# Four cross-attention layers on one core: the next group's projections moved into a PSUM bank of their own ahead of the feed-forward, and attention outputs produced transposed in 32-column strips

## What is computed

```python
# layer 0: per token, heads mix with heads; relu feed-forward, norm after each sum
# layer 1: quantised attention (queries, keys, weights and values rounded to 8 bits)
x = x + qattn(ln(x), ln(x)); x = x + qattn(ln(x), ctx); x = x + geglu_ffn(ln(x))
# layer 2: norm after each sum
logits = qh @ kh.T / sqrt(16) + mask * -1e9
attn1 = mha(x, x, x, look_ahead);       out1 = ln(x + attn1)
attn2 = mha(ctx, ctx, out1, padding);   out2 = ln(out1 + attn2)
x = ln(out2 + relu(out2 @ w1 + b1) @ w2 + b2)
# layer 3: norm ahead of each part
x = x + attn(ln(x), ctx, mask=None)
x = x + attn(ln(x), ln(x), mask=drop)   # masked keys get -inf
x = x + gelu(ln(x) @ w1 + b1) @ w2 + b2
```

## Time and profile before

| | |
|---|---|
| runs | 2275.02, 2273.48, 2274.74 us; median 2274.74 |
| profiled execution | 2274.92 us, span 2273.2 us |
| mean granted TensorE clock | 0.899 of full speed |
| TensorE matmul busy | 1921.8 us, 85% of the span |
| VectorE busy | 1307.1 us, 57% |
| ScalarE busy | 967.8 us, 43% |
| GpSimd busy | 996.9 us, 44% |

### The profile page before, as it was taken

One profiled execution on the slowest core, in us unless ns is written; L12 is line 12 of the kernel. 1 busy time (PEld: TensorE's weight loads), 2 busy tenths in 40 slices (PEclk: granted clock), 3 DMA queues, 4 the chain that ended last, 5 costly groups with the idle time before them and its releaser, 6 DMA issues.

```text
span 2273.2 us, 32499 instructions
## 1 busy us (share of the span) xinstructions
PE 1921.8 (85%) x10497; PEld 1507.4 (66%) x10497; DVE 1307.1 (57%) x2218; ACT 967.8 (43%) x2274; POOL 996.9 (44%) x1235
## 2 busy tenths in 40 slices
PE   4666667677887887887999899998988999999997
PEld 3565556454664655664777677777766787787776
DVE  5877778658558558658444465454533635436361
ACT  1111221224334333334546465564644665556563
POOL 5566665535335336345333454434533423333330
PEclk8889998677877887887999999999988999999999
DMA  7100000000200000000000200000000000000000
GB/s 216 69 5 5 9 5 5 5 1 6 79 1 5 5 0 5 5 0 5 6 1 6 79 0 9 0 5 5 1 5 5 6 6 0 5 23 0 9 1 10
DMA packets 31292, 34.88 MB, mean 15 GB/s; under 512 B 3196, under 2 KB 30040, under 8 KB 30808
## 3 DMA queue, kind: packets, MB, share of 16 engines
q1 hardware_dynamic: 31192, 33.70, 4.8%
HBM read 31.60 MB, written 2.10 MB: 15 GB/s over the span
## 4 chain that ended last, share of the span: by engine, by line
PE 60%; DVE 11%; issue 4%; POOL 2%; ACT 2%; DVEq 0%; POOLq 0%; ACTq 0%
PE ps L503 31%; PE ps L670 9%; PE ps L701 8%; PE ps L680 6%; PE ps L514 3%; DVE xn L874 2%; DVE rowmax L1010 1%; DVE rowsum L1016 1%; PE ps L696 1%; PE ps L668 1%; DVE work L1012 1%; DVE work L1004 1%; DVE O L845 1%; POOL x_all L1126 1%; DVE stats L864 0%
## 5 line engine op out<-in xcount | busy, mean ns | idle before, releaser
L503 PE MATMUL ps<-hT,w_slot 128*128 128x256 f32 x1856 | 455.1, 399 | 21.1 <-ACT hT L744 21.1
L503 PEld LDWEIGHTS ps<-hT,w_slot 128*128 128x128 f32 x1856 | 359.7, 199 | 77.8 <-ACT hT L744 24.0
L1190 POOL TENSOR_TENSOR work<-KT,own_head 128x512 f32<-128x512 f32 x256 | 261.5, 1047 | 288.6 <-ACT KT L756 234.3
L680 PEld LDWEIGHTS ps<-ident,work 128*128 128x128 f32 x1536 | 206.4, 154 | 178.3 <-issue 110.6
L670 PE MATMUL ps<-work,QT 128*128 128x512 f32 x512 | 276.5, 622 | 22.8 <-POOL work L1190 20.6
L680 PE MATMUL ps<-ident,work 128*128 128x128 f32 x1536 | 265.5, 301 | 35.6 <-POOL work L1199 35.6
L1199 POOL TENSOR_SCALAR work<-work,winv 128x128 f32<-128x128 f32 x512 | 184.9, 384 | 218.9 <-DVE winv L1029 218.4
L886 DVE TENSOR_TENSOR x_all<-ps,x_all 128x512 f32 (+1 forms) x88 | 60.7, 690 | 379.6 <-PE ps L503 326.9
L829 ACT ACTIVATE work<-work,rowmax 128x128 f32<-128x128 f32 x768 | 245.0, 392 | 68.1 <-DVE rowmax L1008 66.5
L701 PEld LDWEIGHTS ps<-V,work 128*128 128x128 f32 x2048 | 251.2, 192 | 7.4 <-issue 4.4
L701 PE MATMUL ps<-V,work 128*128 128x17 f32 x2048 | 248.9, 254 | 2.4 <-ACT work L818 2.4
(11 more groups left out here) (119 smaller groups left out, 3015.6 us busy)
## 6 DMA issues: line engine op xcount, KB each, us to landing
ctx_in<-in_ctx SPq DMA_DIRECT2D x32, 256.0 KB, 2.7
w_slot<-in_L_xattn_W SPq DMA_DIRECT2D x2, 1024.0 KB, 6.4
w_slot<-in_L_xattn_ff_w SPq DMA_DIRECT2D x1, 2048.0 KB, 11.2
w_slot<-in_L_xattn_ffn_w SPq DMA_DIRECT2D x2, 1024.0 KB, 9.9
w_slot<-in_L_xattn_w SPq DMA_DIRECT2D x2, 1024.0 KB, 9.3
out<-x_all SPq DMA_DIRECT2D x8, 256.0 KB, 2.1
x_all<-in_x SPq DMA_DIRECT2D x1, 1536.0 KB, 11.7
pad<-in_mask_Bx1x1xS_fk SPq DMA_DIRECT2D x1, 1024.0 KB, 6.7
```

The lines of the kernel that those rows point to most:

```text
L503: mm = pe.matmul(dst, lhsT(k), rhs(k), start=(k == 0), stop=(k == chunks - 1))
L680: mm = pe.transpose(bank(2 + u % 2)[:, tok(h)], prob[u % NP][:, tok(h)], ident[:, :])
L1190: pool.tensor_tensor(KB[u % NK].rearrange("p (h k) -> p h k", h=HU), keys, own_head[:, half * HU:(half + 1) * HU].unsqueeze(2).broadcast_t ...
```

## The change

**Transposed outputs (`direct`), in layers 2 and 3.** The values step now takes 32 columns of a zero-padded `Vz` (two heads of a pair, the other's columns zero) as weights and streams 128 columns of the transposed exponentials: four f32 matmuls per unit that go in turn to two 32-column strips of the array, into one bank (`o_bank`, bank 4) for both sequences. What comes out is transposed already, so `ot` and its copy are gone. Nothing sums the weights any more: VectorE gets a reduction over 128x512 for each unit (`row_sums`, line 1099), one reciprocal of 128x32 and one copy of it to 128x512 columns (lines 1104, 1112), TensorE transposes that (`inverse_rows`, line 751, four transposes at step 11), ScalarE copies it to `inv_T` at step 12, and VectorE multiplies bank 4 by it at step 12 (line 1121, 128x512). `turn(0)` of the next phase waits for `inv_T_ready`. In the quantised layer the two scalings of 128x256 become one of 128x512 at step 12.

**The next group's start, in layers 1 to 3.** `join` is replaced by `ending`: the next group's pieces are put at fixed early slots, in bank 5 (`third`), each waiting until the one ahead of it has been read out of that bank. Layer 0 keeps `join`.

**The feed-forward.** `f0` and `f1` share a slot, `f2` and `f3` the next, and so on, and `y2` is cut into four parts, two to a slot, with `sum` behind the last. In layer 0 this puts the second reduction at line 974 ahead of `sum` on VectorE; before, `sum` stood between the two.

```diff
-        return [("ot", 1), ("y", 0), ("sum", 1)]
+        return [("y", 0), ("sum", 1)] if "direct" in arg else [("ot", 1), ("y", 0), ("sum", 1)]
...
-        return [(f"f{f}", (f % 2 == 2 - 1) + 0 * (f == n - 1)) for f in range(n)] + [("y2", 0), ("sum", 1)]
+        return [(f"f{f}", 0.5) for f in range(n)] + [(f"y2{n}", 0.5) for n in range(Y2)] + [("sum", 1)]
...
+START_SLOT = {"ctx": 1, "stage": 0, "norm": 0, "scale": 0, "tin": 2, "bias": 4, "k": 3, "q": 4, "v": 5}
...
+            def ending(layer, g, after, st):
+                following = {k: STARTING[after[0]][k] for k in SHIFTED} if after else {}
+                pieces = [(int(spot) + 1, emit_piece(layer, g, st, False, following), piece, arg, n)
+                          for piece, spot, arg, n in PLAN[layer][-1]]
+                if not after:
+                    return pieces
+                behind = {k: -ENDING[layer][k] for k in SHIFTED}
+                first = [(START_SLOT[piece], emit_piece(*after, st, True, behind), piece, arg, n) for piece, _, arg, n in PLAN[after[0]][0]]
+                return first + pieces
...
+                left, right = (third, third) if aside else (one, other)
...
+                        if aside:
+                            pe.wait_ge(q["k_ready"], C * (use("att", layer, g, n["att"]) + 1))
+                        else:
+                            pe.wait_ge(q["yadd_done"], G * use("yadd", layer, g, n["yadd"]))
...
+                    if u == 0 and not quant:
+                        pe.wait_ge(s["inv_T_ready"], np_)
...
+                    if not quant and i == U + 4:
+                        act.wait_ge(s["inv_ps"], np_ + 1)
+                        act.activation(inv_T, bank(2), ACT.Copy).then_inc(s["inv_T_ready"], 1)
...
+                def row_sums(u):
+                    dve.wait_ge(s["exp_ready"], U * ap + u + 1)
+                    dve.tensor_reduce(rowsums[:, u * HU:(u + 1) * HU], prob[u % NP].rearrange("p (h k) -> p h k", h=HU), AX.X, ALU.add)\
+                        .then_inc(s["nsums_ready"], 1)
...
+                    if not quant and 0 <= i - SUMS_AT < U:
+                        row_sums(i - SUMS_AT)
+                        if i - SUMS_AT == U - 1:
+                            all_inverses()
+                    if i == U + 4:
+                        outputs()
```

More of the change, by code:

```diff
@@ L129 @@
 PLAN = [layer_plan(layer) for layer in range(NL)]
+SHIFTED = ("norm", "tin", "bias", "post")
+STARTING = [{k: PLAN[layer][1][2][k] for k in SHIFTED} for layer in range(NL)]
+ENDING = [{k: PER_PASS[k][layer] - PLAN[layer][-1][0][3][k] for k in SHIFTED} for layer in range(NL)]
+START_SLOT = {"ctx": 1, "stage": 0, "norm": 0, "scale": 0, "tin": 2, "bias": 4, "k": 3, "q": 4, "v": 5}
 def join(layer, after, end, start):
@@ L311, in use, with use_shifted @@
             return g * n + (BEFORE[kind][layer] + k)
+        def use_shifted(shift, kind, layer, g, k):
+            return use(kind, layer, g, k + shift.get(kind, 0))
         def phase(kind, layer, g, mix, st):
@@ L375, in attend @@
             def attend(layer, g, st, mix, pieces):
                 kind, arg, n = PLAN[layer][2 * mix + 1]
-                together(emit_mix(kind, layer, g, st, arg, n, mix), STEPS_OF[kind], pieces, late)
+                step = emit_mix(kind, layer, g, st, arg, n, mix)
+                together({i: partial(step, i) for i in range(STEPS_OF[kind])}, pieces, late)
             def one_pass(layer, g, after):
-                n_mix = len(PLAN[layer]) // 2
-                for m in range(n_mix):
-                    if m:
-                        attend(layer, g, 0, m, chain(layer, g, 1, m))
-                    attend(layer, g, 1, m, joined(layer, g, after, 0) if m == n_mix - 1 and after else chain(layer, g, 0, m + 1))
+                if len(PLAN[layer]) == 3:
+                    attend(layer, g, 1, 0, joined(layer, g, after, 0))
+                    attend(*after, 0, 0, joined(layer, g, after, 1))
+                    return
@@ L392, in passes @@
+            together({}, chain(0, 0, 0, 0), late)
             attend(0, 0, 0, 0, chain(0, 0, 1, 0))
@@ L644, in emit_mix @@
                 mp = phase("mix", layer, g, mix, st)
-                width = DH + 1
                 lag = ATT_LAG[quant]
+                np_ = None if quant else phase("natt", layer, g, mix, st)
                 def scores(u):
@@ L711, in step @@
                         values(i - lag - 1)
+                    if not quant and i == INVERSE_AT:
+                        inverse_rows()
                 return step
@@ L721, in _, with emit_piece @@
         def _(act):
-            def emit_piece(layer, g, st):
+            def emit_piece(layer, g, st, aside=False, shift={}):
                 q = c[st]
+                left, right = (third, third) if aside else (one, other)
+                due = partial(use_shifted, shift)
                 def emit(piece, arg, n):
@@ L852, in emit @@
                     if piece == "norm":
-                        k = use("norm", layer, g, n["norm"])
+                        k = due("norm", layer, g, n["norm"])
                         if n["yadd"]:
```

242 lines of the change are left out of this document (132 added, 110 removed), and 2 rows, old and new, of the table STEPS.

## The result

| | before | after |
|---|---|---|
| median | 2274.11 us (2272.25 to 2275.02, 4 runs) | 2345.35 us (2344.71 to 2356.75, 4 runs) |
| ratio to before | | 1.0326, 95% interval 1.0294 to 1.0358 |
| span of the profiled execution | 2273.2 | 2343.0 |
| mean granted clock | 0.899 | 0.898 |

What follows compares the result with a forecast made beforehand. TensorE was taken to bind layers 2 and 3, TensorE and VectorE in turn layer 1. Terms 5 - 8 + 38 - 6 + 12 + 9 = +50, less about 2 for clock, on 2274.92 gave 2323 us; range 2268 to 2368.

Steps and rivals of the forecast that it cites:

- End of a long phase in layer 2: Layer 2: k, q and v leave the norm chain's side, TensorE idles about 10 us; +6.3 per long phase, +38 for six.
- The clock: Layer 2, behind the long gap: first scores run at the lower clock, +0.7 us per long phase.
- Strips: Values step in layers 2 and 3: 0.71 us with entry, at half overlap; -0.10 per unit, -0.8 per phase.
- Rival (b): Strips do not overlap at all: 1.0 us per values step, +0.3 for 160 steps, 2371 us; chance 0.15.
- (a): Strips run fully side by side: each values step saves up to 0.38 us, total 2276 or 2258 us; chance 0.15.
- Row sums: Layer 2's eight masked short phases: sums on VectorE delay `xn`, stall 2.7 us instead of 0.4; +1.45 each, +12.
- The last group's long phases: Two long phases at the border to layer 3: -9 from the chain, +6 of moved work; -3 each, -6.
- Layer 1: Quantising moved early makes f0 later by 6 to 7 us, but the phase's tail and start wait go; -8 in all.
- rival (d): Layer 1: quantising k waits in a ring of one bank; +4 us per long phase, 2345 us; chance 0.15.
- Layer 3: Strips, row-sum stalls, norm and `scale` ahead of the feed-forward's transposed input, one chain fewer at the end; +9 us.
- Layer 0: `sum` stands behind the second reduction on the norm's chain; +0.7 us for seven joined phases, +5.
- `y2` cut: Last values step goes between the parts of `y2` in layer 2's long phases: +0.8 us, 0.1 of it given back.

Runs made afterwards that it cites:

- number 3: Changed kernel with the next phase's first three key spreads on GpSimd ahead of the root and `post`, in layer 2's long phases and borders: 2308.92 us.
- number 12: number 10 with the row sums put back at steps 2 to 9, where the change has them: 2294.29 us.
- Number 11: number 10 with the next phase's first three key spreads ahead of `post` on GpSimd, in layer 2 except its border to layer 3: 2221.36 us.
- number 8: Changed kernel with both pairs of a unit in the same 32-column strip, one after another: 2429.69 us.
- number 10: Changed kernel with the next group's start back at its old place, row sums at steps 5 to 9 and `y2` in one slot: 2248.19 us.
- number 7: Changed kernel with the four parts of `y2` in one slot again: 2323.28 us.
- 9: Changed kernel with early key spreads in layer 2, row sums at steps 5 to 9 and `y2` in one slot: 2256.43 us.

## Why the prediction was right, and where its terms were off

**Sign and size.** Slower, inside the range, 22 us above the likeliest time. The gap that was forecast is there: with k, q and v gone from beside the norm chain, TensorE idles 8.56 us in place of 3.41. The runs show its cause twice. With the spread ahead of the chain it closes (number 3, 40.0 us of layer 2), and with k, q and v back beside the chain it is 3.41 us again (number 12). But how the 71 us are made up was forecast less well, and the closeness of the sum is in part luck. By the ledger, moving k, q and v costs layer 2 only 9.8 us, where the forecast had 5.46 for each of six phases and -6 at the border, 27; the transposed outputs with their early sums cost it 22.8, where the forecast had some 8 (12 in the short phases, and 0.55 - 0.44 - 0.7 in each of six long ones); the cut of `y2` costs 22 us in all, where it had 9.

The phases show it too. From the first record of one `scores(0)` to that of the next (lines 670 and 713), the change summed over the phases of a kind (the layers' times above end at a `y2`, so that their sums differ from these at the borders):

| phases | before | after | change | forecast |
|---|---|---|---|---|
| layer 2, six long | 44.6 and 46.1 each | 49.1 and 50.6 each | +26.6 | +38 |
| layer 2, two long at the border to layer 3 | 53.1, 53.6 | 53.0, 52.3 | -1.4 | -6 |
| layer 2, eight short | 26.1 to 28.6 | 26.7 to 29.2 | +14.7 | +12 |
| layer 3, six long | 40.6 and 40.7 each | 41.9 to 46.1 | +17.0 | +7.2 |
| layer 3, eight short | 25.3 to 26.2 | 25.1 to 28.5 | +8.4 | +3.4 |

**End of a long phase in layer 2.** Forecast +6.3 each and a wait of about 10 us; measured +4.4 and 8.56. The chain was to be 0.55 longer and is 0.5 shorter (9.16 against 9.65). The multiplication by the inverses does lengthen it: the statistics start at 1420.53, 2.0 us behind `y2`, where they started 1.6 behind it before. But `scale` is quicker. Before, a bias addition on GpSimd stood beside it, and the forecast left out that this moves to an earlier slot with the other pieces of the start (that the one slowed the other is read from these rows, no run tests it):

```profile
1396.72 1.27 POOL L1139 TENSOR_TENSOR x_all<-x_all,rows 128x512 f32 x1
1396.90 1.56 DVE L874 TENSOR_SCALAR xn<-x_all,meanvar,rstd 128x256 f32 x2 [1.35 <-POOL rstd L1119]
```

```profile
1422.95 0.73 DVE L933 TENSOR_SCALAR xn<-x_all,meanvar,rstd 128x256 f32 x2 [1.35 <-POOL rstd L1195]
```

Per pass, two long and two short phases, I had 2 x 6.3 + 2 x 1.45 = 15.5; it is 13.9.

**The clock.** I added 0.7 us per long phase. In a pass the time outside TensorE's waits fell by 1.4; the strips (0.16 for each of 32 units, 5.1) and the transposes (four times 0.44 gone, four times some 0.5 added) should have taken away 4.9. About 3.5 per pass, an estimate, is the lower clock, 1.7 for each long gap: the term was less than half of what it should have been. The profile shows where: 3.77 us for the first four score records behind the gap, where a short phase has 1.88. Number 11, whose pass has the same work on TensorE at a clock of 1.00, spends 127.1 us outside its waits, against 133.1 here.

**Strips.** Forecast 0.71 for the step with its entry, against 0.81 before. The transposes now take 0.53 to the strips' start (0.44 before) and the step 0.56: 1.09 in place of 1.25, a gain of 0.16 where I took 0.10. Of the two bounds, 1.0 is what one strip gives (0.99, number 8) and 0.43 was not reached. Rival (b) is out, and so is (a) as it was priced, though the step lies nearer to its bound than half overlap does. The price of (a) didn't follow from its own terms: 0.38 for each step of twenty phases is 61 us, not 46. What I had not seen is how much the gain is worth when nothing else is in the way: number 10, 25 us faster than before.

**Row sums.** The stall of the masked short phases in layer 2 was forecast at 2.7 and is 2.46. TensorE and VectorE there, after the change:

```profile
1494.08 0.66 PE L547 MATMUL ps<-ident,xn 128*128 128x128 f32 x4 [2.46 <-DVE xn L933]
```

```profile
1491.35 0.69 DVE L1072 TENSOR_REDUCE rowmax<-work 128x4 f32<-128x512 f32 x1
1491.95 0.68 DVE L1099 TENSOR_REDUCE rowsum<-work 128x4 f32<-128x512 f32 x1
1492.54 1.48 DVE L933 TENSOR_SCALAR xn<-x_all,meanvar,rstd 128x256 f32 x2
```

But the short phases of layer 2 grew by 14.7 us in all, 1.8 each, where I had 1.45: in a full pass the first by 3.0 (it also starts at the lower clock, behind the gap) and the second by 2.0. The second stall of a pass ends with TensorE at the lower clock, as its transposes show, 1.09 us where the first has 0.66, and that falls on what follows. The term failed in size, being too low, and in kind, in its restriction to short phases: in the old order the long ones pay too (number 12).

**The last group's long phases** were to gain 3 each, 9 at their ends against 6 of moved work. The ends came out as forecast: the 19 and 20 us from `y2` to `scores(0)`, with a wait for `xn` of 8.8 us in each, became 9.3 and 9.2, with a wait of 8.7 and 8.6 for the spread keys. But the phases as a whole changed by only -0.1 and -1.3 us, so that the rest of them grew by 10 and not by 6.

**Layer 1** was -8 in the forecast and is +6.4 in this profile, and higher in the others with the same code. The old placement with `y2` in one slot gives 690.9, 691.3 and 691.9 us (numbers 10 to 12), the new one 696.8 and 697.5 (numbers 7 and 9): it costs 5 to 6 us there. From `y2` to `y2`, a pass went from 171.6 to 174.1 us, its waits on TensorE from 32.4 to 37.0. A long phase of layer 1 on TensorE, after the change:

```profile
909.88 1.12 PE L547 MATMUL ps<-ident,xn 128*128 128x128 f32 x4 [2.72 <-DVE xn L933]
...
913.46 3.46 PE L534 MATMUL ps<-hT,w_slot 128*128 128x256 f32 x8 [1.93 <-ACT hT L797]
...
918.89 1.99 PE L534 MATMUL ps<-hT,w_slot 128*128 128x256 f32 x8 [1.05 <-DVE QKb L908]
...
924.77 1.97 PE L534 MATMUL ps<-w_slot,hT 128*128 128x256 f32 x8 [2.65 <-DVE QKb L908]
```

These four waits are 8.4 us. The last two, 3.7, are the ring of rival (d): with one bank for k, q and v, each product waits until VectorE has quantised the one ahead, and VectorE's part stands in its queue among the units' shifts. The first two are for the next group's `xn` and for its transposed copy, which stand early in the phase now. In turn the waits of the first scores for the quantised operands, 5.4 us a pass before, are down to 0.9. So (d), 2345 us with a chance of 0.15, did happen, at about half of its price: a pass is 2.5 us longer where I had 1.8 shorter, 2.2 more per long phase where (d) had 4. That the total came to 2345 too is a coincidence. The step "f0 is later by 6 to 7, the tail of 7.4 and 1 us of start wait go" failed in its first half; these waits of TensorE were not in it.

**Layer 3** was forecast +9 and is +14.5. The placement costs 15.9 us there (number 7 against number 12), where I had put +1.8 and +0.6 for each of three phases, 7.2, for norm and `scale`. It is not the ring: in a pass (2017.42 to 2157.57 us in number 7) no product waits for bank 5. In a pass TensorE waits 11.5 us in number 7 and 6.1 in number 12, and the new waits are for the next group's `xn` (2.0 and 3.4 in the two long phases) and for ScalarE's exponentials (2.4). The mechanism was the forecast's, its size less than half. In turn the rest came out lower: -2.0 for the transposed outputs with early sums, where I had +1.4.

**Layer 0**: +5 forecast, +3.2 measured in this profile, +7 by the median of the eight with the same code.

**`y2` cut.** It cost 22 us; the terms that I had for it in layer 2 (0.8 less 0.1 in six phases) and in layer 0 (5) make 9. In layer 2 it is 1.5 us per place, not 0.7, since the multiplication by the inverses comes ahead of the statistics by it; in layer 0 some 9 us.

So the sum came out near the time through errors of opposite sign: the six long phases of layer 2 were put too high (38 for 27, the moved work too high and the cut too low), and the border, the short phases, layer 1 and layer 3 too low. Two slips of adding are small beside these: the end of the program is put at -1 and goes into layer 3's sum as -2, and layer 1's items make -8.8. The forecast's last step, "less about 2 for the clock that layer 1 and 2 share", had no row behind it and should not have stood there.

## What to carry to other kernels

Before work is moved to an earlier place to get it out of the way, look at what it lies beside: work that fills a chain of other engines is free where it is, and moving it turns it into waiting unless the end of that chain is moved too (here a wait of 3.4 us became 7.1 for 5.5 us of work moved, number 7 against number 12). Here the cheap edit was the other one: not k, q and v, but the one operation that the next phase needs (the key spread) put ahead of `post`, which the next phase doesn't need at once (2248 to 2221 us).

An operation added to an engine with room should stand behind that engine's next urgent hand-over; the same 256 reductions ahead of `scale` cost 46 us in one order and 18 in the other, against their place behind it. And of a change with several parts each should be timed alone: this one held a gain of 25 us under losses of 46, 29 and 22.

## What the runs showed of the hardware

Four f32 matmuls of 128 columns with 32-column weights take 0.99 us in one strip and 0.56 in two, from start to start; the hand-over from full-width transposes to strips takes 0.09 more than to full-width matmuls (0.53 against 0.44). An exponential on ScalarE that accumulates its row sum is followed by a read of 0.19 us (0.22 in unmasked phases). `scale` over 128x256 on VectorE takes 0.40 to 0.41 us in the 71 places of the kernel after where GpSimd is idle, or nearly so, beside it, and between 0.40 and 1.29 where GpSimd works throughout; what makes the difference among the latter these runs don't settle. Gaps of 2.4 us on TensorE were followed by the lower clock in some phases and not in others (the transposes behind it at 1.09 us against 0.66); what tells the two apart these runs don't settle either.
